# Rotary queries and keys projected once for four heads, halves placed by DMA, probabilities scaled on VectorE

## The chip, the cores and the metric

The kernel runs on one core of a Trainium2 chip. Its engines are TensorE (PE, with its weight loads as PEld), VectorE (DVE), ScalarE (ACT), GpSimd (POOL) and SyncE (SP, which issues DMAs); each works through its own instructions in order and waits on semaphores. The metric is the time of one execution on the device in microseconds (us).

## The reference

A decoder layer over x of shape (8, 256, 128): self-attention, cross-attention to a context of 1601 tokens, then a block with rotary attention and a mixture of 31 experts. The change is in the rotary attention alone. Cut to it:

```python
H, HD = (16, 64)
xn = _rmsnorm(x, gamma1)
q = (xn @ q_w + q_b).reshape(b, s, H, HD).transpose(0, 2, 1, 3)
k = (xn @ k_w + k_b).reshape(b, s, H, HD).transpose(0, 2, 1, 3)
v = (xn @ v_w + v_b).reshape(b, s, H, HD).transpose(0, 2, 1, 3)
# _rope: angles = arange(s)[:, None] * theta
x1, x2 = (x[..., 0::2], x[..., 1::2])
concatenate([x1 * cos - x2 * sin, x1 * sin + x2 * cos], axis=-1)   # for q and for k
scores = einsum('bhqd,bhkd->bhqk', q, k) / sqrt(HD)     # causal
attn = softmax(scores, axis=-1)
ctx = einsum('bhqk,bhkd->bhqd', attn, v)
attn_out = ctx @ o_w + o_b + xn
```

There are 8 batches of 256 tokens and 16 heads of 64 columns; everything here is float32.

## The kernel before

The program is a sequence of stages, each a block with one instruction stream per engine: self-attention, cross-attention, rotary attention (`rotary_attention`, from L1449), the gates, and the experts. The tables of sines and cosines (`RotaryTables`, L218) and the reordered weights are prepared during the self-attention stage.

In the rotary stage a unit is a pair of heads, `UN` = 8 units to a batch, 64 in all. The order is written out: `program` (L1493) calls `slot` for each engine once per unit, and within a slot each engine works on several units at different stages, set by the lags of L1433: the projection of the slot's own unit, the scores of the unit two slots back, its normalisation three back, its transposes four back, and its values five back. Slots 1 to 3 of a batch also carry the three parts of the norm of the next batch (`ahead`), slot 5 the output product of the batch before (item "o"), slot 6 its end on VectorE (`finish`), and slots 1, 2, 6 and 7 one piece each of the values' projection (item "v").

What the engines do for a unit:

- TensorE projects (L1764): queries and keys, each with the weights `w1` and with `w2`, where even and odd columns have changed places, 128 rows (two heads) by 256 tokens. Each of these 4 matmuls is 2 passes in the trace, 8 in all.
- VectorE (L1631) adds the bias and multiplies each of the four by the table: four products of 256 columns, from PSUM.
- GpSimd (L1554, L1557) adds them in pairs into `qT` and `kT`.
- TensorE makes the scores and adds the mask (L1723, L1726); VectorE takes the row maxima (L1607, L1608); ScalarE makes the exponentials and their sums (L1666); VectorE the reciprocals (L1613).
- GpSimd scales the probabilities by the reciprocals, four instructions over `prob` (L1548), one slot before TensorE transposes them (L1752). ScalarE copies the transposes (L1677), TensorE multiplies by the values (L1742), ScalarE copies the result (L1672).

In a slot TensorE's order is: "v" item, scores, "o" item, values, transposes, projection. SP issues nothing in this stage after the loads of the experts' first weights.

## Time and profile before

| | us |
|---|---|
| median of 3 runs (1802.65 to 1806.12) | 1804.21 |
| the profiled execution | 1805.63 |
| its span | 1803.6 |
| TensorE matmul busy | 1581.4 (88%) |
| VectorE busy | 1118.3 (62%) |
| ScalarE busy | 905.3 (50%) |
| GpSimd busy | 556.2 (31%) |

The profile shows one execution. Busy time is summed over the whole span, and the stages differ: the rotary stage lies between about 1132 and 1535 us of it. What a change in it is worth is read from the waits and the timeline of that stage.

### The profile page before, as it was taken

The page shows a single profiled execution, that of the slowest core. Times are in us where ns is not written, and L with a number is a line of the kernel's source. Part 1 is how long each engine was busy: PE and PEld are TensorE (multiplying, and loading weights), DVE is VectorE, ACT ScalarE, POOL GpSimd, SP SyncE. Part 2 cuts the span into 40 slices and gives each one's busy share as a digit, 9 for nine tenths or more (in the row PEclk, how much of TensorE's full clock was granted, in tenths as well). Part 3 has the DMA queues.
Part 4 walks back from the last instruction along what each step waited for, and adds up shares of the span by engine and source line. Part 5 has one row for each costly group of instructions (what it writes and reads, how often), then busy time and mean ns, then how long its engine had stood idle before and what let it go on. Part 6 is the DMA issues. An engine that isn't in the chain of part 4 may idle for free. (4 is left out here: it accounts for less than half of the span.)

```text
span 1803.6 us, 29464 instructions
## 1 busy us (share of the span) xinstructions
PE 1581.4 (88%) x11021; PEld 845.3 (47%) x11045; DVE 1118.3 (62%) x2537; ACT 905.3 (50%) x1612; POOL 556.2 (31%) x690
## 2 busy tenths in 40 slices
PE   1677776699999999999999999799999997499999
PEld 1344443244444444444444444466666675344444
DVE  4755542577778686868777784556666663355554
ACT  1233333076666667676666667255555554234333
POOL 4010102020111203030302000577888885133332
PEclk9978886599999999999999999899999998599999
DMA  4222211603232323223222320000000000000001
GB/s 102 69 51 54 54 37 55 114 5 93 47 96 47 97 47 96 47 77 52 63 53 43 97 33 2 8 1 2 1 1 1 1 1 1 7 20 22 22 19 36
DMA packets 88417, 75.32 MB, mean 42 GB/s; under 512 B 24724, under 2 KB 78388, under 8 KB 87348
## 3 DMA queue, kind: packets, MB, share of 16 engines
q1 hardware_dynamic: 88276, 73.44, 18.5%
q8 instruction: 88, 1.44, 0.3%
q14 instruction: 53, 0.43, 0.1%
HBM read 42.73 MB, written 30.42 MB: 41 GB/s over the span
## 5 line engine op out<-in xcount | busy, mean ns | idle before, releaser
L1137 DVE TENSOR_REDUCE b_chunk_max<-psum 128x1 f32<-128x400 f32 (+1 forms) x1024 | 545.4, 570 | 206.4 <-PE psum L1352 199.0
L1275 ACT ACTIVATE b_prob<-psum 128x1024 f32<-128x1024 f32 (+1 forms) x416 | 425.6, 1023 | 238.5 <-PE psum L1389 234.4
L1352 PE MATMUL psum<-k_stack,q_stack 128*128 128x400 bf16 (+1 forms) x1024 | 318.3, 345 | 31.2 <-DMA k_stack<-b_k_scratch 12.2
L1361 PE MATMUL psum<-b_prob,b_v_aug 128*32 128x256 f32 (+1 forms) x3328 | 266.1, 391 | 1.8 <-ACT b_prob L1275 0.5
L1389 PE MATMUL psum<-q_stack,k_stack 128*128 128x256 bf16 (+1 forms) x1664 | 253.0, 275 | 0.3 <-DMA q_stack<-b_mparts 0.3
L1389 PEld LDWEIGHTS psum<-q_stack,k_stack 128*128 128x128 bf16 (+1 forms) x1664 | 146.3, 99 | 118.1 <-issue 51.2
L1548 POOL TENSOR_SCALAR c_prob<-c_prob,c_rec 128x128 f32<-128x128 f32 (+1 forms) x256 | 191.9, 767 | 8.9 <-POOL c_kT L1557 8.3
L2027 DVE TENSOR_TENSOR e_hg<-e_gl,e_gate 128x512 f32<-128x512 f32 x128 | 123.9, 986 | 113.0 <-PE psum L2042 69.3
L1352 PEld LDWEIGHTS psum<-k_stack,q_stack 128*128 128x128 bf16 x1024 | 99.2, 97 | 201.7 <-DVE b_chunk_max L1137 170.5
L1631 DVE SCALAR_TENSOR_TENSOR c_turned<-psum,c_bias,c_tab 128x256 f32<-128x256 f32 x256 | 106.1, 476 | 111.1 <-PE psum L1764 111.1
L1666 ACT ACTIVATE c_prob<-psum,c_mneg 128x128 f32<-128x128 f32 (+1 forms) x256 | 104.1, 418 | 136.4 <-DVE c_mneg L1608 136.4
L2008 ACT ACTIVATE e_gl<-psum,b1T 128x512 f32<-128x512 f32 x128 | 87.8, 687 | 139.8 <-PE psum L2055 131.6
L2042 PE MATMUL psum<-e_hg,e_w 128*128 128x512 f32 x256 | 131.9, 598 | 8.6 <-DVE e_hg L2027 8.6
L2055 PE MATMUL psum<-anT,e_w 128*128 128x512 f32 x256 | 133.3, 604 | 1.4 <-PEq L1813 1.4
L1764 PE MATMUL psum<-c_xT,c_w 128*128 128x256 f32 x512 | 130.6, 401 | 1.7 <-DVE c_turned L1631 1.2
L1993 POOL PARTITION_BROADCAST e_gate<-e_gate_row x32 | 73.8, 2311 | 174.4 <-DMA e_gate_row<-gates 139.9
L1071 POOL COPY b_v_aug<-b_v_new 128x768 f32<-128x768 f32 (+1 forms) x32 | 15.9, 528 | 335.1 <-issue 268.5
L1361 PEld LDWEIGHTS psum<-b_prob,b_v_aug 128*32 128x32 f32 (+1 forms) x3328 | 65.8, 108 | 105.4 <-issue 86.7
L1764 PEld LDWEIGHTS psum<-c_xT,c_w 128*128 128x128 f32 x512 | 98.1, 202 | 15.4 <-DVE c_turned L1631 2.5
L578 DVE TENSOR_REDUCE a_mneg<-psum 128x2 f32<-128x512 f32 (+1 forms) x96 | 65.0, 688 | 58.9 <-PE psum L752 57.6
L653 ACT ACTIVATE a_prob<-psum 128x1024 f32<-128x1024 f32 x64 | 51.8, 811 | 72.1 <-PE psum L723 70.9
L2042 PEld LDWEIGHTS psum<-e_hg,e_w 128*128 128x128 f32 x256 | 49.0, 192 | 71.0 <-issue 52.8
(213 smaller groups left out, 1961.6 us busy)
## 6 DMA issues: line engine op xcount, KB each, us to landing
k_stack<-b_k_scratch SPq DMA_DIRECT2D x32, 600.4 KB, 10.5
b_k_scratch<-b_kparts SPq DMA_DIRECT2D x7, 1200.8 KB, 4.3
b_k_scratch<-b_kparts SPq DMA_DIRECT2D x7, 800.5 KB, 6.0
b_ctx<-in_ctx SPq DMA_DIRECT2D x8, 576.0 KB
e_w<-in_L_ffn_re_w SPq DMA_DIRECT2D x62, 64.0 KB, 1.9
a_scratch<-a_parts SPq DMA_DIRECT2D x16, 192.0 KB, 2.2
k_stack<-a_scratch SPq DMA_DIRECT2D x16, 192.0 KB, 4.9
q_stack<-b_q_scratch SPq DMA_DIRECT2D x32, 96.0 KB, 2.2
```

Source lines behind the costliest of these rows:

```text
L1137: nc.vector.tensor_reduce(out=chunk_max[:, half, q, column4(hh), c:c + 1], in_=psum[:, 2 + u % 2, 0:w], axis=AX.X, op=ALU.max).then_inc(ma ...
L1275: nc.scalar.activation(prob[0:k, buf, :].rearrange("p (a c) -> p a c", a=2), psum[0:k, 4 + 2 * buf:6 + 2 * buf, :], ACT.Exp, scale=HD ** - ...
L1352: nc.tensor.matmul(psum[:, 2 + u % 2, 0:hi - lo], queries_of(qst, h, slice(q * P, q * P + P)), keys_of(kst, h, slice(lo, hi)), start=True, ...
L1361: last = nc.tensor.matmul(pv[32 * hh:32 * hh + 32, :], v_aug[0:k, kt, g * GH + hh, :], prob[0:k, buf, c:c + T], start=(kt == 0), stop=(kt ...
L1389: lastmm = nc.tensor.matmul(psum[0:k, 4 + 2 * buf + hh % 2, (hh // 2) * T:(hh // 2) * T + T], keys_of(kst, h, slice(n * P, n * P + k)), qu ...
L1548: ins = nc.gpsimd.tensor_scalar(prob[:, w % PB, hh, lo:hi], prob[:, w % PB, hh, lo:hi], rec[:, w % PB, hh, q:q + 1], None, ALU.mult)
L1631: ins = nc.vector.scalar_tensor_tensor(out=turned[:, u % 2, m, w, :], in0=bank[:, w * T:(w + 1) * T], scalar=bias[:, m, w, u:u + 1], in1=t ...
L1666: ins = nc.scalar.activation(prob[:, u % PB, hh, lo:hi], psum[:, 2 + hh, lo:hi], ACT.Exp, bias=mneg[:, par, q, hh:hh + 1], accum_out=total ...
L1764: last = nc.tensor.matmul(bank[:, w * T:(w + 1) * T], weights[:, m, u * P:(u + 1) * P], xT[:], start=True, stop=True)
L2027: nc.vector.tensor_tensor(hg[:, k % BUFS, :], gl[:, k % BUFS, :], gate[j][:, c * TW:(c + 1) * TW], ALU.mult)\
L2042: nc.tensor.matmul(psum[:, c, :], w[:, j, 1, :], hg[:, buf, :], start=second.start, stop=False).then_inc(y_done, 1)
L2055: nc.tensor.matmul(psum[:, 4 + k % BUFS, :], w[:, j, 0, :], d["anT"][:, c * TW:(c + 1) * TW], start=True, stop=True)\
```

## The change

A unit of the projection is now queries (even units) or keys (odd units) of four heads: one matmul gives the first columns of the four heads' pairs (`half` 0), one the second (`half` 1), 32 columns a head. The weights and biases come in this order from the host, so the copies on GpSimd (`order_weights`) and the small bias loads are gone. VectorE makes four products out of the two projections (first times cosine, second times sine, first times sine, second times cosine). GpSimd adds the last two into `second` and subtracts the first two twice, into two slots of `qT` or `kT` that take two heads each. Half of the rows written there belong to the other slot's heads; SP's four DMAs of 32 rows put the `second` halves in their place. The scores of a unit wait for the DMAs of queries and keys of its four heads (`placed`) and come three slots after the projection instead of two. The reciprocals and the scaling of the probabilities are both on VectorE, at the start of the slot in which TensorE transposes them.

```diff
-        self.w1, self.w2 = sb("c_w1", [P, 2, CH * CD]), sb("c_w2", [P, 2, CH * CD])
+        self.w = sb("c_w", [P, 2, UN // 2, 2, P])
...
-        for q in range(0, P, 64):
-            link(nc.vector.tensor_scalar(tab[q:q + 32, 1, 1, :], tab[q:q + 32, 1, 1, :], -1.0, None, ALU.mult))
...
-                tables.order_weights(pool)
-
...
-SCORES_LAG, NORM_LAG, TURN_LAG, VALUES_LAG = 2, 3, 4, 5
+SCORES_LAG, TURN_LAG, VALUES_LAG = 3, 4, 5
...
@@ -1513,6 +1496,13 @@
         @block.sync
         def _(sp):
             experts_pre.load(sp)
+            for n in range(B * UN):
+                m, u, buf = n % 2, n % UN // 2 * 2, n % 2
+                sp.wait_ge(turned_ready, n + 1)
+                for pos in range(4):
+                    to = 32 * (pos ^ 1)
+                    sp.dma_start((qT, kT)[m][to:to + 32, u + pos % 2, :], second[32 * pos:32 * pos + 32, buf, :])\
+                        .then_inc(placed[m], 16)
@@ -1539,24 +1529,24 @@
-                w = c_unit(n, NORM_LAG, first, drain)
-                if w is not None:
-                    pool.wait_ge(rec_ready, T_.up("weigh"))
-                    pool.sem_inc(passed, 1)
-                    for hh in range(2):
-                        for lo, hi, q in ((0, P, 0), (P, 3 * P, 1)):
-                            ins = nc.gpsimd.tensor_scalar(prob[:, w % PB, hh, lo:hi], prob[:, w % PB, hh, lo:hi],
-                                                          rec[:, w % PB, hh, q:q + 1], None, ALU.mult)
-                    ins.then_inc(weighed, 1)
                 if u is not None:
-                    pool.wait_ge(terms_ready, T_.up("unit"))
-                    par = u % 2
-                    nc.gpsimd.tensor_tensor(qT[:, u, :], turned[:, par, 0, 0, :], turned[:, par, 0, 1, :], ALU.add)\
-                        .then_inc(own_pool, 1)
+                    v = T_.up("unit")
+                    pool.wait_ge(terms_ready, v)
+                    m, g, t4 = u % 2, u // 2 * 2, terms[:, u % 2]
+                    if v > UN:
+
+                        pool.wait_ge(s_full, (v - 1) // 2 * 2 + 2 - UN)
+                    if v > 2:
+
+                        pool.wait_ge(placed[m], 64 * ((v - 1) // 2))
+                    nc.gpsimd.tensor_tensor(second[:, m, :], t4[:, 2, :], t4[:, 3, :], ALU.add).then_inc(own_pool, 1)
                     pool.wait_ge(own_pool, T_.up("own_pool"))
-                    nc.gpsimd.tensor_tensor(kT[:, u, :], turned[:, par, 1, 0, :], turned[:, par, 1, 1, :], ALU.add)\
-                        .then_inc(turned_ready, 1)
-                    pool.wait_ge(turned_ready, T_.now("unit"))
+                    for j in range(2):
+                        nc.gpsimd.tensor_tensor((qT, kT)[m][:, g + j, :], t4[:, 0, :], t4[:, 1, :], ALU.subtract)\
+                            .then_inc((own_pool, turned_ready)[j], 1)
+                        if j == 0:
+                            pool.wait_ge(own_pool, T_.up("own_pool"))
+                    pool.wait_ge(turned_ready, v)
@@ -1600,6 +1590,16 @@
             def slot(i, n, first, drain, ahead):
+                u = c_unit(n, TURN_LAG, first, drain)
+                if u is not None:
+                    dve.wait_ge(exp_done, T_.up("weigh"))
+                    own(nc.vector.reciprocal(rec[:, u % PB].rearrange("p h q -> p (h q)"),
+                                             total[:, u % PB].rearrange("p h q -> p (h q)")))
+                    for hh in range(2):
+                        for lo, hi, q in ((0, P, 0), (P, 3 * P, 1)):
+                            ins = nc.vector.tensor_scalar(prob[:, u % PB, hh, lo:hi], prob[:, u % PB, hh, lo:hi],
+                                                          rec[:, u % PB, hh, q:q + 1], None, ALU.mult)
+                    ins.then_inc(weighed, 1)
...
-                    for m, bank in enumerate((q_bank, k_bank)):
-                        for w in range(2):
-                            ins = nc.vector.scalar_tensor_tensor(out=turned[:, u % 2, m, w, :], in0=bank[:, w * T:(w + 1) * T],
-                                                                 scalar=bias[:, m, w, u:u + 1], in1=tab[:, m, w, :],
-                                                                 op0=ALU.add, op1=ALU.mult)
+                    m, bank = u % 2, (q_bank, k_bank)[u % 2]
+                    for dst, (half, wave) in enumerate(((0, 0), (1, 1), (0, 1), (1, 0))):
+                        ins = nc.vector.scalar_tensor_tensor(out=terms[:, m, dst, :], in0=bank[:, half * T:(half + 1) * T],
+                                                             scalar=bias[:, m, u // 2, half:half + 1], in1=tab[:, m, wave, :],
+                                                             op0=ALU.add, op1=ALU.mult)
                     ins.then_inc(terms_ready, 1)
@@ -1715,7 +1710,9 @@
-                    pe.wait_ge(turned_ready, T_.up("scores"))
+                    quads = (T_.up("scores") + 1) // 2
+                    pe.wait_ge(placed[0], 64 * quads)
+                    pe.wait_ge(placed[1], 64 * quads)
@@ -1758,11 +1755,11 @@
-                    wait(pe, terms_ready, T_.now("unit", 1))
-                    for m, bank in enumerate((q_bank, k_bank)):
-                        for w, weights in enumerate((w1, w2)):
-                            last = nc.tensor.matmul(bank[:, w * T:(w + 1) * T], weights[:, m, u * P:(u + 1) * P], xT[:],
-                                                    start=True, stop=True)
+                    wait(pe, terms_ready, T_.now("unit", 2))
+                    bank = (q_bank, k_bank)[u % 2]
+                    for half in range(2):
+                        last = nc.tensor.matmul(bank[:, half * T:(half + 1) * T], qkw[:, u % 2, u // 2, half, :], xT[:],
+                                                start=True, stop=True)
                     last.then_inc(proj_full, 1)
```

VectorE before, one plain slot of the rotary stage, from the products of one unit (`c_turned`) to those of the next; `c_mneg` holds the negated row maxima, `c_rec` the reciprocals:

```order
L1631 SCALAR_TENSOR_TENSOR c_turned<-psum,c_bias,c_tab 128x256 [waits c_turned_ready,c_proj_full]
L1631 SCALAR_TENSOR_TENSOR c_turned<-psum,c_bias,c_tab 128x256 x3
L1607 TENSOR_REDUCE c_mneg<-psum 128x2 [waits c_s_full]
L1608 TENSOR_REDUCE c_mneg<-psum 128x2
L1613 RECIPROCAL c_rec<-c_total 128x4 [waits c_exp_done]
L1631 SCALAR_TENSOR_TENSOR c_turned<-psum,c_bias,c_tab 128x256 [waits c_turned_ready,c_proj_full]
L1631 SCALAR_TENSOR_TENSOR c_turned<-psum,c_bias,c_tab 128x256 x3
```

VectorE after, the same place (`c_terms` are the four products, `c_prob` the probabilities):

```order
L1626 SCALAR_TENSOR_TENSOR c_terms<-psum,c_bias,c_tab 128x256 [waits c_turned_ready,c_proj_full]
L1626 SCALAR_TENSOR_TENSOR c_terms<-psum,c_bias,c_tab 128x256 x3
L1596 RECIPROCAL c_rec<-c_total 128x4 [waits c_exp_done]
L1600 TENSOR_SCALAR c_prob<-c_prob,c_rec 128x128 [waits c_own_dve]
L1600 TENSOR_SCALAR c_prob<-c_prob,c_rec 128x256
L1600 TENSOR_SCALAR c_prob<-c_prob,c_rec 128x128
L1600 TENSOR_SCALAR c_prob<-c_prob,c_rec 128x256
L1607 TENSOR_REDUCE c_mneg<-psum 128x2 [waits c_s_full]
L1608 TENSOR_REDUCE c_mneg<-psum 128x2
L1626 SCALAR_TENSOR_TENSOR c_terms<-psum,c_bias,c_tab 128x256 [waits c_turned_ready,c_proj_full]
L1626 SCALAR_TENSOR_TENSOR c_terms<-psum,c_bias,c_tab 128x256 x3
```

The reciprocal has moved in front of the row maxima, and four scalings stand between it and them.

TensorE before, a slot from the scores (`c_kT,c_qT`) and the mask over the values (`c_probT,c_v`) and the transposes (`ident,c_prob`) to the projection (`c_xT,c_w`):

```order
L1723 MATMUL psum<-c_kT,c_qT 128x128 [waits c_exp_done,c_turned_ready]
L1723 MATMUL psum<-c_kT,c_qT 128x128
L1723 MATMUL psum<-c_kT,c_qT 128x256 x2
L1726 MATMUL psum<-mask_qk,identb 128x2x128 x2
L1742 MATMUL psum<-c_probT,c_v 64x256 [waits c_att_ready,c_probT_ready]
L1742 MATMUL psum<-c_probT,c_v 64x256
L1742 MATMUL psum<-c_probT,c_v 64x128 x2
L1752 MATMUL psum<-ident,c_prob 128x128 [waits c_probT_ready,c_weighed]
L1752 MATMUL psum<-ident,c_prob 128x128 x5
L1764 MATMUL psum<-c_xT,c_w 128x256 [waits c_terms_ready]
L1764 MATMUL psum<-c_xT,c_w 128x256 x3
```

TensorE after, the same place:

```order
L1720 MATMUL psum<-c_kT,c_qT 128x128 [waits c_exp_done,c_k_placed,c_q_placed]
L1720 MATMUL psum<-c_kT,c_qT 128x128
L1720 MATMUL psum<-c_kT,c_qT 128x256 x2
L1723 MATMUL psum<-mask_qk,identb 128x2x128 x2
L1739 MATMUL psum<-c_probT,c_v 64x256 [waits c_att_ready,c_probT_ready]
L1739 MATMUL psum<-c_probT,c_v 64x256
L1739 MATMUL psum<-c_probT,c_v 64x128 x2
L1749 MATMUL psum<-ident,c_prob 128x128 [waits c_probT_ready,c_weighed]
L1749 MATMUL psum<-ident,c_prob 128x128 x5
L1761 MATMUL psum<-c_xT,c_w 128x256 [waits c_terms_ready]
L1761 MATMUL psum<-c_xT,c_w 128x256
```

The order of the groups stays. The scores wait for the two `placed` semaphores, and the projection has two matmuls instead of four.

## Rows read from the trace of the kernel before

**Rows 1.** Busy time by windows, a batch: stretch, its length, each engine, granted clock, DMA.
```profile
1374.00:1420.00 46.00, 42.69 (x292) 30.36 (x294) 28.91 (x87) 24.70 (x85) 37.64 (x54) 1.00 0.00 1
```

**Rows 2.** Waits from 1200 to 1480: who for whom, us in total, times, longest.
```profile
DVE c_turned L1631 <- PE psum L1764: 84.1, 37, 5.2
```

**Rows 3.** The projection: its timeline row in slot 4, then all of its passes.
```profile
1160.34 1.89 PE L1764 MATMUL psum<-c_xT,c_w 128*128 128x256 f32 x8
...
L1764 PE MATMUL psum<-c_xT,c_w x512: 378/379/795, 1139.2 to 1504.5; 128*128 128x256 f32 x171
```

**Rows 4.** Timeline, slots 4 and 5: start, duration, engine, line, operation, count [idle before].
```profile
1296.73 1.66 DVE L1631 SCALAR_TENSOR_TENSOR c_turned<-psum,c_bias,c_tab 128x256 f32<-128x256 f32 x4 [5.02 <-PE psum L1764]
...
1298.48 0.72 POOL L1554 TENSOR_TENSOR c_qT<-c_turned 128x256 f32<-128x256 f32 x1 [0.46 <-DVE c_turned L1631]
...
1298.71 0.87 PE L1752 MATMUL psum<-ident,c_prob 128*128 128x128 f32 x6
...
1299.42 1.89 PE L1764 MATMUL psum<-c_xT,c_w 128*128 128x256 f32 x8
...
1301.24 0.93 PE L1723 MATMUL psum<-c_kT,c_qT 64*128 64x128 f32 x8
...
1301.35 1.66 DVE L1631 SCALAR_TENSOR_TENSOR c_turned<-psum,c_bias,c_tab 128x256 f32<-128x256 f32 x4 [1.94 <-PE psum L1764]
...
1302.33 3.74 PE L1704 MATMUL psum<-c_ow,c_attT 128*128 128x128 f32 x32
1302.92 0.41 DVE L1607 TENSOR_REDUCE c_mneg<-psum 128x2 f32<-128x256 f32 x1
...
1303.85 0.17 DVE L1613 RECIPROCAL c_rec<-c_total 128x4 f32<-128x4 f32 x1
1303.97 0.37 ACT L1666 ACTIVATE c_prob<-psum,c_mneg 128x128 f32<-128x128 f32 x1 [1.83 <-DVE c_mneg L1608]
...
1305.48 0.21 ACT L1666 ACTIVATION_READ_ACCUMULATOR c_prob<-psum,c_mneg 128x1 f32 x1
...
1305.99 0.87 PE L1742 MATMUL psum<-c_probT,c_v 128*64 128x256 f32 x8
```

**Rows 5.** Timeline, norm scalings beside GpSimd's adds; then the two apart (ns min/median/max).
```profile
1285.46 0.73 POOL L1554 TENSOR_TENSOR c_qT<-c_turned 128x256 f32<-128x256 f32 x1
...
1285.95 1.13 DVE L127 TENSOR_SCALAR xn<-x_sb,mv,rstd 128x128 f32<-128x128 f32 x2
...
1286.26 0.73 POOL L1557 TENSOR_TENSOR c_kT<-c_turned 128x256 f32<-128x256 f32 x1
...
L127 DVE TENSOR_SCALAR xn<-x_sb,mv,rstd x2: 324/602/881, 1285.9 to 1286.2; 128x128 f32<-128x128 f32 x2
```

**Rows 6.** Groups by line and form: a 256-column multiplication by a per-partition scalar.
```profile
L303 DVE TENSOR_SCALAR t_ang<-t_pos,c_theta 128x256 f32<-128x256 f32 x2 | 0.7, 354 | 0.1
```

**Rows 7.** Timeline, four small DMAs and who waits for them; then issues by size.
```profile
1106.84 2.37 SPq L994 DMA_DIRECT2D q_stack<-b_mparts  x4
...
1110.27 0.61 PE L1389 MATMUL psum<-q_stack,k_stack 128*128 128x256 bf16 x4 [0.32 <-DMA q_stack<-b_mparts]
...
a_scratch<-a_parts SPq DMA_DIRECT2D x16, 192.0 KB, 2.2
```

**Rows 8.** Timeline, VectorE: last of the norm's second part; first and last of a batch's end.
```profile
1288.44 0.17 DVE L142 TENSOR_SCALAR ve<-msq 128x2 f32<-128x2 f32 x1
...
1312.50 1.23 DVE L149 SCALAR_TENSOR_TENSOR an_cur<-c_o,rstd,c_rows 128x128 f32<-128x128 f32 x2
...
1314.60 0.65 DVE L1587 TENSOR_TENSOR x_sb<-x_sb,c_o 128x256 f32<-128x256 f32 x1
```

**Rows 9.** Timeline after a gap of TensorE; then a window as in rows 1.
```profile
1292.55 0.87 PE L1752 MATMUL psum<-ident,c_prob 128*128 128x128 f32 x6 [2.35 <-POOL c_prob L1548]
...
1293.26 3.43 PE L1764 MATMUL psum<-c_xT,c_w 128*128 128x256 f32 x8
...
262.50:269.00 6.50, 3.94 (x43) 1.87 (x42) 3.69 (x10) 2.34 (x5) 0.00 (x0) 1.00 0.00 1
```

More of the change, by code:

```diff
@@ L249, in scratch @@
     def scratch(self, sb):
-        self.raw = sb("t_raw", [P, 2, CH * CD])
         self.pos, self.posi = sb("t_pos", [P, T]), sb("t_posi", [P, T], mybir.dt.int32)
@@ L256, in load @@
         nc, a = self.nc, self.a
-        for m, name in enumerate(("q_w", "k_w")):
-            sp.dma_start(self.raw[:, m, :], a["L0_ffn_" + name]).then_inc(self.loaded, 16)
-        with nc.allow_non_contiguous_dma(reason="biases are spread over partitions once"):
-            for quarter in range(4):
-                rows = slice(32 * quarter, 32 * quarter + 32)
-                sp.dma_start(self.theta[rows, :], a["L0_ffn_theta"].rearrange("(p a) -> p a", a=1)).then_inc(self.loaded, 16)
-                hh, par = quarter // 2, quarter % 2
-                for m, name in enumerate(("q_b", "k_b")):
-                    v = a["L0_ffn_" + name].rearrange("(j h f a) -> h a f j", j=UN, h=2, a=2)
-                    for w in range(2):
-                        sp.dma_start(self.bias[rows, m, w, :], v[hh, (par + w) % 2]).then_inc(self.loaded, 16)
-    N_LOADS = 2 + 4 * 5
+        for m, name in enumerate(("q", "k")):
+            sp.dma_start(self.w[:, m].rearrange("p g a n -> p (g a n)"), a["L0_ffn_%s_w" % name]).then_inc(self.loaded, 16)
+            sp.dma_start(self.bias[:, m].rearrange("p g a -> p (g a)"), a["L0_ffn_%s_b" % name]).then_inc(self.loaded, 16)
+        for quarter in range(4):
+            rows = slice(32 * quarter, 32 * quarter + 32)
+            sp.dma_start(self.theta[rows, :], a["L0_ffn_theta"].rearrange("(p a) -> p a", a=1)).then_inc(self.loaded, 16)
+    N_LOADS = 2 * 2 + 4
     def positions(self, pool):
         self.nc.gpsimd.iota(self.posi[:], pattern=[[1, T]], base=0, channel_multiplier=0).then_inc(self.pos_set, 1)
-    def order_weights(self, pool):
-        pool.wait_ge(self.loaded, 16 * self.N_LOADS)
-        for m in range(2):
-            v = self.raw[:, m, :].rearrange("p (g f a) -> p g a f", g=CH, a=2)
-            for par in range(2):
-                for dst, src in ((self.w1, par), (self.w2, 1 - par)):
-                    self.nc.gpsimd.tensor_copy(dst[:, m, :].rearrange("p (g a f) -> p g a f", g=CH, a=2)[:, :, par], v[:, :, src])
     def angles(self, dve):
@@ L1461, in sem @@
             return ctx.enter_context(nc.semaphore(name))
-        w1, w2, tab, bias = tables.w1, tables.w2, tables.tab, tables.bias
+        qkw, tab, bias = tables.w, tables.tab, tables.bias
         vw, ow, rows, vbT, w_loaded = tables.vw, tables.ow, tables.rows, tables.vbT, tables.w_loaded
@@ L1466, in rotary_attention @@
         o = sb("c_o", [P, QT, D])
-        turned = sb("c_turned", [P, 2, 2, 2, T])
+        terms = sb("c_terms", [P, 2, 4, T])
+        second = sb("c_second", [P, 2, T])
         qT = sb("c_qT", [P, UN, T])
@@ L1487, in rotary_attention @@
         misc, pv_bank = psum[:, 6, :], psum[:, 7, :]
-        PER = dict(unit=UN, scores=UN, weigh=UN, turn=UN, values=UN, item=6, batch=1, norm=3, out=1, own_pool=UN,
-                   own_dve=(NORM_LINKS + RMS_LINKS) + RMS_LINKS + 3)
+        PER = dict(unit=UN, scores=UN, weigh=UN, turn=UN, values=UN, item=6, batch=1, norm=3, out=1, own_pool=2 * UN,
+                   own_dve=(NORM_LINKS + RMS_LINKS) + RMS_LINKS + 3 + UN)
         N_W = tables.N_W
@@ L1609, in slot @@
                         .then_inc(m_ready, 1)
-                u = c_unit(n, NORM_LAG, first, drain)
-                if u is not None:
-                    dve.wait_ge(exp_done, T_.up("weigh"))
-                    nc.vector.reciprocal(rec[:, u % PB].rearrange("p h q -> p (h q)"), total[:, u % PB].rearrange("p h q -> p (h q)"))\
-                        .then_inc(rec_ready, 1)
                 ahead()
@@ L2093 @@
     for name in _NAMES:
-        v = _np.ascontiguousarray(inputs[name])
+        v = _np.asarray(inputs[name])
+        if name in ("L0_ffn_q_w", "L0_ffn_k_w"):
+            v = v.reshape(D, 4, 2, 2, 32, 2).transpose(0, 1, 5, 3, 2, 4).reshape(D, CH * CD)
+        if name in ("L0_ffn_q_b", "L0_ffn_k_b"):
+            v = v.reshape(4, 2, 2, 32, 2).transpose(2, 1, 3, 0, 4).reshape(P, UN)
+        v = _np.ascontiguousarray(v)
         arrays["in_" + name] = v
```

6 lines of the change are left out of this document (3 added, 3 removed).

## The prediction

> **What bounds the kernel now.** I read the page first: TensorE is the busiest engine and the stages follow each other, so a change in one stage is worth what it does there. The changed lines run in the rotary stage. The table by windows shows a batch of it: of 46.0 us TensorE is busy 42.69, VectorE 28.91, GpSimd 37.64, at a full clock [rows 1]. The table of waits says the same from the other side: VectorE waits for the projection 84.1 us in 280 [rows 2], so it has room on average. From the first projection of the steady stretch (slot 4 of the first batch) to the last one, whose eighth pass starts at 1504.5, are 1504.5 - 1.5 - 1160.3 = 343 us for 59 slots, 5.8 us a slot [rows 3]. TensorE sets that; GpSimd, which scales the probabilities a whole slot before they are transposed, is nearly hidden.
>
> The timeline of single slots then gives the pieces [rows 4]: transposes 0.71 us until the projection starts (1298.71 to 1299.42); projection 1.89 for 8 passes, with 0.378 for one by itself [rows 3], so (1.89 - 0.378) / 7 = 0.216 a pass; VectorE starts 0.04 after it and needs 1.66 for its four products; GpSimd starts 0.09 after those; scores and mask 1.09 (1301.24 to 1302.33), output product 3.66 (to 1305.99), values 0.87; row maxima 1.0 (1302.92 until the exponentials start); reciprocal 0.17; exponentials 1303.97 to 1305.69, 1.7.
>
> **What the change takes away.** Half of the projection: 4 passes of 8 in each of 64 slots, 4 x 0.216 = 0.86 us a slot, 55 us of TensorE's path. GpSimd loses four scalings a slot and gets a third add. In the self-attention stage GpSimd's reordering of the weights goes, which stood beside VectorE's work there; I estimate 1 us for it.
>
> **What it adds: a loop of one slot.** Before, the scaling of a unit was done in the slot before its transposes. Now it is in the same slot, on VectorE, in front of the row maxima and the products; TensorE's transposes wait for it, and the projection stands behind the transposes (both orders are shown above). So each slot runs around: products of slot n-1 end, scaling, transposes, projection of slot n, products of slot n. No engine can run ahead of this. Outside the scaling it costs 0.06 (a wake, estimated between the 0.04 and 0.09 above) + 0.71 + projection 3 x 0.216 + 0.378 = 1.03 + 0.04 + 1.66 = 3.5 us.
>
> The scaling by itself: a 128-column scaling by per-partition scalars takes 0.32 at least [rows 5], a 256-column one 0.354 [rows 6]; 2 x (0.32 + 0.354) = 1.35, with the reciprocal 1.5 us. Bounds for it alone: 1.1 (if the pieces overlap as the row maxima do) and 1.9 (if a 256-column piece ran at the products' 1.66 / 4 = 0.42 and small ones too). Alone, the loop is 5.0 us.
>
> It isn't alone. GpSimd's three adds start 0.09 us after the products end, which is when VectorE goes on to the scaling. What happens when a scaling from SBUF meets GpSimd adds stands in one place of the trace: two equal scalings, 0.324 and 0.881 us; the first ends at 1286.27, just behind the add that ended at 1286.19; the second ends at 1287.08, behind the add of 1286.26 to 1286.99 [rows 5]. The adds kept their 0.73. So the scaling waits for the whole add and gets in between two. The Trainium skill has this as a rule (SBUF — State Buffer, Who interferes with whom): one port pair is shared by VectorE and GpSimd and is locked for a whole instruction. The trace agrees with it here; without such a lock the sum would be that of the first rival.
>
> With three adds at a pitch of 0.80 (ends at 0.82, 1.62 and 2.42 after the products), three scalings end at some 0.9, 1.7 and 2.5, and the fourth is free: 2.5 + 0.35 = 2.9 us. Loop: 2.9 + 3.5 = 6.4 us. Bounds: 5.0 (never in the way) and 7.3 (all four behind the last add: 2.42 + 1.35 = 3.8 instead of 2.9). I take 6.4, by the row. The exponentials are ready: they end 1.7 after the maxima, the products 1.66 after them at the earliest.
>
> **The transfers.** Four DMAs of 32 KB start when the third add ends, 2.42 after the products; the scores two slots on wait for them, in every odd slot. Four small DMAs issued together take 1106.84 to 1110.27, 3.4 us, until TensorE goes on [rows 7]; one alone takes 2.2 from issue to landing [rows 7]. For 32 KB each I take 3.6 for all four. Ready 6.1 us after the products; scores 1.09 and values 0.87 bring the transposes to 8.1. The scaling of that slot lets them go at 6.4 + 2.9 = 9.3. So the transfers are hidden by the locked loop, except where the output product (3.66, slot 5) stands between: 6.1 + 1.09 + 3.66 + 0.87 = 11.7, 2.3 us late, once a batch. If the loop were the short one, this wait would take its place.
>
> **VectorE's other work.** Between maxima and products there is 0.06 + 0.71 + 1.03 + 0.04 - 1.0 = 0.8 us of room. The second part of the norm took 1285.95 to 1288.61, the end of a batch 1312.50 to 1315.25 [rows 8], each with about 0.6 of the same lock in it, which no longer falls there: 2.1 and 2.15, so 1.3 and 1.35 stand out. The shorter items fit.
>
> **The sum.** A batch: 8 x 6.4 + 2.3 + 1.3 + 1.35 = 56.2 us, 8 x 5.8 = 46.5 now. The 59 slots are 7 batches and 3 plain slots: 7 x 56.2 + 3 x 6.4 = 412.6, less 343 is 70 us. Filling is a little shorter and draining has one more slot of scores, which waits for a transfer: together I estimate +2. Stage A -1. Together +71. The profiled execution took 1805.6 us for a span of 1803.6, 1.4 over the median of 1804.2; on the median I forecast 1804.2 + 71 = **1875 us**. The 55 us taken off TensorE turn into idle time of TensorE.
>
> **First rival: no lock, the transfers bind.** Loop 5.0, but in odd slots the transposes start at 8.1 instead of 5.0 + 1.5 = 6.5. A pair of slots: 8.1 + 0.71 + 1.03 + 0.04 + 1.66 = 11.5; a batch 4 x 11.5 + 3.66 = 49.8; 7 x 49.8 + 3 x 5.8 = 366, +23: with fill, drain and stage A +24, **1828**. For it: only one clear meeting of the two kinds of instruction is in the trace. Against it: that one is exact to 0.1 us.
>
> **Second rival, on the other side.** No lock, and four transfers land like one, in 2.2 us. Place: the scores of odd slots. Ready at 4.7, transposes at 6.7; a pair is 10.1, a batch 44.1 and some 0.9 for the long items; 7 x 45 + 3 x 5.0 = 330, -13, with the rest -12: **1792**. It decides only if no lock and a landing under some 2.6 us come together: at 2.6 a pair is 10.5, and 4 x 10.5 + 3.66 + 0.9 are the present 46.5 us. Were even the loop wrong and TensorE still the bound, all 55 us would come: 1750; both orders speak against that.
>
> **Third rival: the clock.** TensorE would be busy 3.8 of 6.4 us, with gaps of 1 to 1.7 us. After the 2.35 us gap at 1290.2 the next 8 passes took 3.43 instead of 1.89, so it had fallen to the lower of its levels, 1.2 GHz [rows 9]. Against it: 6.5 us with 3.94 busy went at a full clock [rows 9]. At the low level the loop gets 0.71 + 1.03 = 1.7 us longer and the output product 3.7: some 130 us if always so; TensorE would then be busy over 7 of 8.1 us, which should bring the clock back, so I count half: **1940**. [...]
>
> **How the numbers follow.** Locked loop at a full clock: 55%, own range 1855 to 1900. No lock: 20%. Clock: 17%. The fast one: 4%. The rest, 4%, lies around no change, when errors of a microsecond a slot in the loop add up. The range of 8 in 10 reaches from 1820 (the first rival with its width) to 1940. About 0.2% (3.6 us) is what a measurement of this kernel can tell from no change: faster 4%, within it 2%, slower 94%.
>
> **What would show it.** In the profile after: slots of the rotary stage at 6.4 us and a batch at 56; TensorE's transposes idle before them, released by VectorE's scaling, once a slot; VectorE's products waiting for the projection about 0.8 us in plain slots; the four scalings together 2.5 us or more while the adds keep 0.73 (first step); the projection at 4 passes in 1.03; TensorE's scores released by a transfer only in slot 5. If the scalings take 1.4 together, the lock is wrong and the scores of odd slots will be waiting for transfers. If the granted clock of the stage is under 0.9, the third rival has its part. The forecast is wrong if the transposes don't wait for the scaling at all.

## The result, and the profile after

The changed kernel takes 1870.55 us (median of 4 runs, 1869.59 to 1870.9); the kernel before, run beside it, 1805.16 (1802.65 to 1808.79). The ratio is 1.036, 95% interval 1.0341 to 1.0379: 3.6% slower, 65 us. The forecast was 1875. (One execution of one later kernel, with the projection ahead of the transposes, took 3020.89 us in the slow state; its ratio leaves that one out.)

The profiled span is 1868.7 us, 65.1 more than before. The rotary stage has nearly all of it. From the projection of slot 4 of the first batch, which starts at 1157.84, to the last one, at 1563.95, are 406.1 us for 59 slots, against 343 [rows 3]: +63. Slot 4 itself comes 2.5 us earlier (1160.34 before), and from the start of the last projection to the gates' first transposes it is 36.7 us (to 1600.63) instead of 32.3 (1503.03 to 1535.36).

Two windows of the profile after, columns as in rows 1; the first is one batch, from the start of one output product to the next:

```profile
1436.38:1491.01 54.63, 40.41 (x267) 27.28 (x267) 43.43 (x120) 24.96 (x85) 22.21 (x29) 0.94 0.07 20
...
1170.00:1500.00 330.00, 244.44 (x1590) 165.48 (x1592) 260.04 (x712) 149.53 (x510) 132.63 (x173) 0.93 0.07 20
```

This batch takes 54.6 us instead of 46; the six between the output products at 1212.54 and 1545.34 take 54.0 to 57.7, 55.5 in the mean. TensorE idles 14 us of the batch shown and VectorE has become the busier engine. The granted clock of the stage is 0.93, where the same window of the kernel before has 0.98. From the costliest groups and the DMA issues of the page:

```profile
L1720 PE MATMUL psum<-c_kT,c_qT 64*128 64x128 f32 (+1 forms) x512 | 65.1, 374 | 84.9 <-DMA c_kT<-c_second 75.7
...
L1749 PE MATMUL psum<-ident,c_prob 128*128 128x128 f32 x384 | 63.7, 309 | 34.8 <-DVE c_prob L1600 34.6
...
c_qT<-c_second SPq DMA_DIRECT2D x128, 32.0 KB, 1.8
```

TensorE waits for both new things: 35 us in front of the transposes for the scaling, and 76 us in front of the scores for the transfers, where the forecast had such a wait in slot 5 alone. The forms of the scaling apart, from 1170 to 1500 (busy us, mean ns):

```profile
L1600 DVE TENSOR_SCALAR c_prob<-c_prob,c_rec 128x128 f32<-128x128 f32 x95 | 72.5, 764 | 1.7
L1600 DVE TENSOR_SCALAR c_prob<-c_prob,c_rec 128x256 f32<-128x256 f32 x94 | 32.1, 341 | 0.0
```

The 128-column scaling takes over twice as long as the 256-column one that follows it: the time is a wait. The timeline, slots 7 and 0, then the first half of a locked scaling block of another batch taken apart, then slots 1 and 3 to 5 (start, duration, count, idle before):

```profile
1455.23 1.66 DVE L1626 SCALAR_TENSOR_TENSOR c_terms<-psum,c_bias,c_tab 128x256 f32<-128x256 f32 x4 [0.91 <-PE psum L1761]
...
1457.01 2.02 DVE L1600 TENSOR_SCALAR c_prob<-c_prob,c_rec 128x128 f32<-128x128 f32 x4
...
1460.86 1.66 DVE L1626 SCALAR_TENSOR_TENSOR c_terms<-psum,c_bias,c_tab 128x256 f32<-128x256 f32 x4 [0.90 <-PE psum L1761]
...
1322.84 0.82 DVE L1600 TENSOR_SCALAR c_prob<-c_prob,c_rec 128x128 f32<-128x128 f32 x1
1322.85 0.72 POOL L1542 TENSOR_TENSOR c_second<-c_terms 128x256 f32<-128x256 f32 x1 [3.04 <-DVE c_terms L1626]
...
1322.84 1.08 DVE L1600 TENSOR_SCALAR c_prob<-c_prob,c_rec 128x128 f32<-128x128 f32 x2
1323.65 0.85 POOL L1545 TENSOR_TENSOR c_qT<-c_terms 128x256 f32<-128x256 f32 x1
...
1463.37 0.93 PE L1720 MATMUL psum<-c_kT,c_qT 64*128 64x128 f32 x8 [1.69 <-DMA c_kT<-c_second]
...
1466.99 1.72 PE L1761 MATMUL psum<-c_xT,c_w 128*128 128x256 f32 x4
...
1476.83 0.93 PE L1720 MATMUL psum<-c_kT,c_qT 64*128 64x128 f32 x8 [2.55 <-DMA c_kT<-c_second]
...
1479.88 1.03 PE L1761 MATMUL psum<-c_xT,c_w 128*128 128x256 f32 x4
...
1480.95 1.66 DVE L1626 SCALAR_TENSOR_TENSOR c_terms<-psum,c_bias,c_tab 128x256 f32<-128x256 f32 x4 [0.38 <-PE psum L1761]
...
1485.30 2.41 SPq L1504 DMA_DIRECT2D c_kT<-c_second  x4
...
1486.52 1.66 DVE L1626 SCALAR_TENSOR_TENSOR c_terms<-psum,c_bias,c_tab 128x256 f32<-128x256 f32 x4 [0.91 <-PE psum L1761]
...
1489.03 1.65 PE L1720 MATMUL psum<-c_kT,c_qT 64*128 64x128 f32 x8 [2.54 <-DMA c_kT<-c_second]
...
1491.01 4.34 PE L1699 MATMUL psum<-c_ow,c_attT 128*128 128x128 f32 x32
...
1496.80 1.03 PE L1761 MATMUL psum<-c_xT,c_w 128*128 128x256 f32 x4
...
1497.87 1.66 DVE L1626 SCALAR_TENSOR_TENSOR c_terms<-psum,c_bias,c_tab 128x256 f32<-128x256 f32 x4 [0.33 <-PE psum L1761]
```

The reader is to see three things. A plain slot is 1460.86 - 1455.23 = 5.63 us. Its four scalings go in two pairs: the first, which starts with the add, ends at 1323.66, 0.09 us behind it, and the second is through 0.26 later, at 1323.92. The record of the next add starts at 1323.65 already, but it takes 0.85 us instead of 0.73, so part of it is a wait too. And slot 5 takes 1497.87 - 1486.52 = 11.35 us, because the transfers of its unit, issued at 1485.30, let the scores go at 1489.03 only; the projection's 4 passes there, and in plain slots, take the 1.03 of the forecast. The scores in that slot (1.65) and the output product (4.34, 3.74 before [rows 4]), and transposes and projection of slot 1 (1.54, and 1.72 as shown, against 0.87 and 1.03), ran partly or wholly at TensorE's lower level, 1.2 GHz, each after a wait for a transfer (1.69 us in slot 1, 2.54 in slot 5). The wait of 2.55 us in slot 3 left the clock at full: the projection behind it takes 1.03.

### The profile page after: what moved, and what is told of

Same layout as the page of the kernel before. It is cut to its first block and busy times, and to the rows that moved or that the text cites. A ratio compares the mean times of both kernels' runs of the same rounds, so it can differ in the third digit from the quotient of the medians.

```text
span 1868.7 us, 29303 instructions
## 1 busy us (share of the span) xinstructions
PE 1558.5 (83%) x10789; PEld 815.2 (44%) x10789; DVE 1229.2 (66%) x2791; ACT 903.2 (48%) x1612; POOL 421.6 (23%) x490
## 5 line engine op out<-in xcount | busy, mean ns | idle before, releaser
L1626 DVE SCALAR_TENSOR_TENSOR c_terms<-psum,c_bias,c_tab 128x256 f32<-128x256 f32 x256 | 106.1, 476 | 55.8 <-PE psum L1761 55.8
L1720 PE MATMUL psum<-c_kT,c_qT 64*128 64x128 f32 (+1 forms) x512 | 65.1, 374 | 84.9 <-DMA c_kT<-c_second 75.7
L1600 DVE TENSOR_SCALAR c_prob<-c_prob,c_rec 128x128 f32<-128x128 f32 (+1 forms) x256 | 123.8, 543 | 2.2
L1749 PE MATMUL psum<-ident,c_prob 128*128 128x128 f32 x384 | 63.7, 309 | 34.8 <-DVE c_prob L1600 34.6
L1720 PEld LDWEIGHTS psum<-c_kT,c_qT 64*128 64x128 f32 x512 | 37.7, 200 | 119.6 <-issue 102.4
```

The source lines that it names most:

```text
L1600: ins = nc.vector.tensor_scalar(prob[:, u % PB, hh, lo:hi], prob[:, u % PB, hh, lo:hi], rec[:, u % PB, hh, q:q + 1], None, ALU.mult)
L1626: ins = nc.vector.scalar_tensor_tensor(out=terms[:, m, dst, :], in0=bank[:, half * T:(half + 1) * T], scalar=bias[:, m, u // 2, half:half ...
L1720: nc.tensor.matmul(psum[:, 2 + hh, q * P:q * P + w], qT[r, u, q * P:q * P + P], kT[r, u, 0:w], start=(q == 0), stop=False, tile_position=( ...
```

## The experiments

My theory after the result had three parts: a loop of one slot through the scaling, the lock between VectorE's scalings and GpSimd's adds in it, and the transfers with the low clock behind their waits. Its rivals: that the transfers are hidden, that one part alone has the whole loss, and that any rotation of the loop's order would give the time back. All ratios are to the kernel before, run on the same chip.

**No transfers.** SP issues none, and the scores wait for the adds. The second halves of queries and keys are thus not put in place; everything else is computed.

```diff
-                for pos in range(4):
-                    sp.dma_start((qT, kT)[m][to:to + 32, ...], second[...]).then_inc(placed[m], 16)
...
-                    if v > 2:
-                        pool.wait_ge(placed[m], 64 * ((v - 1) // 2))
...
-                    pe.wait_ge(placed[0], 64 * quads)
-                    pe.wait_ge(placed[1], 64 * quads)
+                    pe.wait_ge(turned_ready, 2 * quads)
```

> The changed kernel without SyncE's four transfers a slot: the second halves are not put in place, so the scores are computed from other numbers; they wait for GpSimd's adds instead. Loop theory (scaling, transposes, projection, products, with the scaling waiting for GpSimd's adds: 5.62 us a slot in the trace of the changed kernel): slots stay at 5.6, but the waits of odd slots and half of the slot with the output product go: a batch 54.6 -> some 49.6, time about 1833. Rival 1, the transfers are hidden (as my forecast had it): no more than 2.3 us a batch, 1853 or above. Rival 2, the transfers bind everything: a slot goes under 5.2, time 1810 or below. If TensorE's clock had fallen because of the waits, the granted clock of the stage rises from 0.93 to 0.98 or more.

Measured: 1825.05 us, ratio 1.0102 (1.0078 to 1.0126), 45 us under the changed kernel. So the transfers were not hidden. Without their waits the granted clock from 1170 to 1500 is 0.98, as in the kernel before. The timeline shows the plain slot unchanged, 5.62 to 5.63:

```profile
1375.16 1.66 DVE L1616 SCALAR_TENSOR_TENSOR c_terms<-psum,c_bias,c_tab 128x256 f32<-128x256 f32 x4 [0.90 <-PE psum L1750]
...
1380.79 1.66 DVE L1616 SCALAR_TENSOR_TENSOR c_terms<-psum,c_bias,c_tab 128x256 f32<-128x256 f32 x4 [0.90 <-PE psum L1750]
```

Of the waits from 1170 to 1500 the scaling's is left alone on TensorE's path, where the changed kernel had 53.0 us for the keys' transfers and 27.6 for the scaling:

```profile
PE psum L1738 <- DVE c_prob L1590: 50.6, 47, 1.8
```

**No transfers, and the adds after the scaling.** As in the last kernel, and GpSimd waits until VectorE's scaling of the slot is done, so that the two never meet.

```diff
+                    if v > 3:
+                        pool.wait_ge(weighed, v - 3)
                     nc.gpsimd.tensor_tensor(second[:, m, :], t4[:, 2, :], t4[:, 3, :], ALU.add)
```

> As no_transfers, and GpSimd's adds of a slot wait until VectorE has done its scalings, so the two never meet. Scores are again computed without the second halves in place. Lock theory: the four scalings take 1.3 instead of 2.0 us, the loop 5.0 instead of 5.6, a batch about 46, time about 1807, 26 us under no_transfers. Rival (no lock, the scalings are slow by themselves): scalings stay at 2.0, time as no_transfers or above it.

Measured: 1783.78, ratio 0.9875 (0.9852 to 0.9898). The lock is worth 41 us of the other kernel's time, more than I expected. The 128-column form, and the timeline:

```profile
L1592 DVE TENSOR_SCALAR c_prob<-c_prob,c_rec 128x128 f32<-128x128 f32 x121 | 34.3, 284 | 2.1
```

```profile
1349.84 1.66 DVE L1618 SCALAR_TENSOR_TENSOR c_terms<-psum,c_bias,c_tab 128x256 f32<-128x256 f32 x4 [0.90 <-PE psum L1752]
...
1351.62 1.01 DVE L1592 TENSOR_SCALAR c_prob<-c_prob,c_rec 128x128 f32<-128x128 f32 x4
...
1354.60 1.66 DVE L1618 SCALAR_TENSOR_TENSOR c_terms<-psum,c_bias,c_tab 128x256 f32<-128x256 f32 x4 [1.04 <-PE psum L1752]
```

Without adds beside them the four scalings take 1.01 us, not 2.02, and the slot 4.76 (4.64 for the next one). The 128-column scaling falls from 766 to 284 ns; the 256-column one takes 348 and took 341.

**The projection ahead of the transposes.** The two groups change places in TensorE's stream, which takes scaling and transposes out of the loop from products to products. The edit in outline:

```diff
-   transposes (waits for weighed); projection (waits for terms_ready)
+   projection (waits for terms_ready); transposes (waits for weighed)
```

> The changed kernel, complete, with TensorE's projection ahead of its transposes in every slot. Loop theory: products of a slot no longer wait for the scaling and the transposes, the one-slot loop is gone; what is left is the pair loop over the transfers: adds end 2.7 after the products, transfers 3.7, scores and values 2.0, projection 1.0, products 1.7, that is 11.1 for two slots; a batch 4 x 11.1 + 3.7 = 48, time about 1822. Rival (the loop was never the bound, only the transfers): 0.7 us less in each odd slot, 3 us a batch, about 1848. If the clock keeps falling, 10 to 20 us more in either.

Measured: 1866.52, ratio 1.0328 (1.0299 to 1.0358), 4 us better than the changed kernel by the medians and hardly more than their spread. The loop theory's 1822 is missed, with 10 to 20 us for the clock too. The rival's 1848 with the same 10 to 20 reaches it (the granted clock from 1170 to 1500 is 0.90), but not for its reason, since in the kernels without transfers the loop does bind. So the rival that a rotation of the order gives the time back is refuted for this one. TensorE's timeline shows why:

```profile
1392.69 0.95 PE L1720 MATMUL psum<-c_kT,c_qT 64*128 64x128 f32 x8 [2.23 <-DMA c_kT<-c_second]
...
1394.11 1.55 PE L1739 MATMUL psum<-c_probT,c_v 128*64 128x256 f32 x8
1395.59 1.75 PE L1752 MATMUL psum<-c_xT,c_w 128*128 128x256 f32 x4
```

The projection of the next slot stands in the same stream behind scores that wait for a transfer. What the shorter loop gives is spent there, and behind each wait TensorE runs slower (1.55 and 1.75 instead of 0.87 and 1.13). In this kernel it waited 66.8 us of 330 for the keys' transfers, against 53.0 in the changed one.

**The kernel before, with the scaling alone moved to VectorE** (in the slot between scores and transposes, ahead of the row maxima as in the change; projection, adds and lags are those of before). In outline:

```diff
-                        nc.gpsimd.tensor_scalar(prob[...], prob[...], rec[...], None, ALU.mult)
+   in VectorE's slot, ahead of the row maxima, of the unit 3 slots back:
+                            ins = nc.vector.tensor_scalar(prob[...], prob[...], rec[...], None, ALU.mult)
```

> The kernel before with one part of the change alone: the scaling is done by VectorE, at the start of the slot before the transposes, so no loop closes over it. Loop theory: VectorE gets some 2 us a slot more work, 4.9 x 8 + 7 = 46 us a batch, just as much as TensorE; time within 1795 to 1815. Rival (the scaling on VectorE costs by itself, wherever it stands): 1850 or above.

Measured: 1835.3, ratio 1.0162 (1.0131 to 1.0194): about 29 us slower, and outside my range of up to 1815; the rival's 1850 was not reached either. The scaling has the same lock here, and it stands in front of the row maxima, for which the exponentials wait, and for these the next scores:

```profile
1329.68 2.03 DVE L1601 TENSOR_SCALAR c_prob<-c_prob,c_rec 128x128 f32<-128x128 f32 x4
...
1332.67 0.37 ACT L1662 ACTIVATE c_prob<-psum,c_mneg 128x128 f32<-128x128 f32 x1 [3.15 <-DVE c_mneg L1609]
...
1334.54 0.93 PE L1719 MATMUL psum<-c_kT,c_qT 64*128 64x128 f32 x8 [1.62 <-ACT c_prob L1662]
```

So this part of the change costs time by itself, even where the transposes come a slot later. That halving the projection cannot give it back while the loop is there is argued from the loop, not tried by itself.

**One more slot of lag.** The changed kernel with scores, transposes and values 4, 5 and 6 slots after the projection, and the items moved to fit. It computes all that the changed kernel does.

```diff
-SCORES_LAG, TURN_LAG, VALUES_LAG = 3, 4, 5
+SCORES_LAG, TURN_LAG, VALUES_LAG = 4, 5, 6
-C_ITEMS = {1: [("v", 0)], 2: [("v", 1)], 5: [("o", 0)], 6: [("v", 2)], 7: [("v", 3)]}
+C_ITEMS = {2: [("v", 0)], 3: [("v", 1)], 6: [("v", 2), ("o", 0)], 7: [("v", 3)]}
```

> The changed kernel, complete, with scores, transposes and values one slot later (4, 5, 6 instead of 3, 4, 5; the pieces of the values' projection and the output product move along). The loop over the scaling and its meeting with GpSimd's adds stay; the transfers get a slot more. Transfer theory: as without the transfers (1825), plus one slot of draining: about 1830, slots at 5.6, no wait of the scores for a transfer. Rival (the four transfers cost something else than the wait, traffic or SyncE): 1850 or above.

Measured: 1830.96, ratio 1.0151 (1.0122 to 1.0179), the expected time within 1 us. I had expected no wait of the scores for a transfer; for the keys' transfers 11.6 us of 53.0 are left in the stretch 1170 to 1500 (second row), while the scaling holds the transposes as before (first row):

```profile
PE psum L1747 <- DVE c_prob L1600: 51.1, 47, 1.8
...
PE psum L1718 <- DMA c_kT<-c_second: 11.6, 17, 1.0
```

**The same, and the adds after the scaling** (`pool.wait_ge(weighed, v - 4)` ahead of them, for v over 4).

> As lag4, and GpSimd's adds wait for VectorE's scalings of the slot, complete. If waits for transfers and the lock were the whole loss: as no_transfers_late_adds (1784) plus a slot of draining and items at another place, about 1790, below the kernel before. Rival (later adds make the transfers late again: adds end 3.6 after the products, ready at 7.3, scores wanted at 9 to 10): the scores of odd slots wait, 1800 or above.

Measured: 1786.26, ratio 0.9906 (0.9876 to 0.9936). This is the fastest complete kernel, 0.9% faster than the kernel before and some 84 us faster than the changed one. Now TensorE's scores wait for a transfer 1.9 us in the stretch (second row), and for the exponentials instead:

```profile
PE psum L1720 <- ACT c_prob L1661: 32.4, 37, 1.9
...
PE psum L1720 <- DMA c_kT<-c_second: 1.9, 4, 0.9
```

**The same, and the projection ahead of the transposes**, to see whether the rotation helps once nothing else binds.

> As lag4_late_adds, with TensorE's projection ahead of its transposes. Now no transfer and no lock stands before the loop, so loop theory says that this is where the order matters: the plain slot falls from 4.6 to VectorE's own work, 0.2 + 1.3 + 1.0 + 1.7 = 4.1 us, a batch by 2 to 4 us, time about 1770. Rival (project_first gave 4 us, so the order doesn't matter here either): within 5 us of lag4_late_adds.

Measured: 1792.24, ratio 0.9929 (0.9905 to 0.9952), 6 us behind the last one instead of 16 ahead; the rival's 5 us is missed too, narrowly. TensorE's timeline:

```profile
1405.10 2.08 PE L1752 MATMUL psum<-c_xT,c_w 128*128 128x256 f32 x4
...
1419.65 0.93 PE L1720 MATMUL psum<-c_kT,c_qT 64*128 64x128 f32 x8 [1.90 <-ACT c_prob L1661]
...
1424.58 0.93 PE L1720 MATMUL psum<-c_kT,c_qT 64*128 64x128 f32 x8 [1.15 <-ACT c_prob L1661]
```

Scores here follow scores by 4.93 us (1419.65 to 1424.58), both times released by the exponentials of the unit before, which read the same PSUM banks: once the projection's loop is open, this one (scores, maxima with the scaling ahead of them, exponentials, scores) holds the slot at the same length; the last kernel has 4.93 for it too (1416.45 to 1421.38). Behind the wait of 1.90 us that ends at 1402.83 projection and transposes took 2.08 and 1.26 instead of 1.13 and 0.82; the granted clock from 1170 to 1450 is 0.96 against 1.00 for the last kernel, which may be what put this one behind it. That the banks are what holds was read, not tried, and the clock's part is argued only.

**The scaling back on GpSimd** in the changed kernel, a slot ahead of the transposes as before (lags 3, 4, 5, 6; items and output product move along as in the kernels with one more slot). In outline:

```diff
-   VectorE: reciprocals and four scalings at the start of the slot
+   VectorE: reciprocals; GpSimd: the four scalings of the unit 4 slots back, ahead of its adds
```

> The changed kernel with the second part of the change undone: GpSimd scales the probabilities, four slots behind the projection, transposes five and values six behind (a slot later than in the changed kernel, as the order before had it); scores stay at three. Transfer theory: the pair loop over the transfers stays (adds 2.4, transfers 3.7, scores and values 2.0, transposes 0.7, projection 1.0, products 1.7: 11.5 for two slots), 50 a batch, about 1825 to 1835. Lock theory alone (all of the loss is VectorE's scaling): back at 1805 or below, the projection's saving would show.

Measured: 1888.51, ratio 1.0466 (1.0438 to 1.0494), far from 1825 to 1835.

```profile
1414.71 1.65 DVE L1628 SCALAR_TENSOR_TENSOR c_terms<-psum,c_bias,c_tab 128x256 f32<-128x256 f32 x4
...
1414.74 2.98 POOL L1538 TENSOR_SCALAR c_prob<-c_prob,c_rec 128x128 f32<-128x128 f32 x4 [0.23 <-POOL c_qT L1554]
...
1417.69 0.73 POOL L1551 TENSOR_TENSOR c_second<-c_terms 128x256 f32<-128x256 f32 x1
...
1420.05 2.41 SPq L1504 DMA_DIRECT2D c_kT<-c_second  x4
...
1423.78 1.65 PE L1722 MATMUL psum<-c_kT,c_qT 64*128 64x128 f32 x8 [4.27 <-issue]
```

VectorE is free, but the adds, whose products are done at 1416.36, stand behind a 3 us scaling on GpSimd until 1417.69. The transfers are issued 3.7 us after the products instead of 2.7, the scores start 3.73 later, and TensorE idles 4.27 us (which the profile puts down to no wait that it shows) and then runs at its lower level: the scores take 1.65, and the granted clock from 1170 to 1500 is 0.86. I had priced the scaling by VectorE's loop alone and forgotten what it does to the transfers behind it.

**TensorE kept busy during the waits.** The changed kernel with matmuls nobody reads in front of the wait of every even unit.

```diff
+                    wait(pe, exp_done, T_.now("scores", 1))
+                    if u % 2 == 0:
+                        for _ in range(36):
+                            nc.tensor.matmul(psum[:, 2, 3 * P:4 * P], t["identb"][:], t["identb"][:], start=True, stop=True)
                     pe.wait_ge(placed[0], 64 * quads)
                     pe.wait_ge(placed[1], 64 * quads)
-                    wait(pe, exp_done, T_.now("scores", 1))
```

> The changed kernel, with 36 extra matmuls (128 columns, bf16, into columns that nobody reads) ahead of TensorE's wait for the transfers in every even unit, so that it is busy for most of that wait; the result is unchanged. Clock theory: after the changed kernel's waits of 2.6 us the output product took 5.37 us instead of 3.7, transposes and projection of slot 1 3.3 instead of 1.9, some 3 to 4 us a batch. With TensorE busy these go: granted clock of the stage 0.97 or more, output product 3.7, batch 51, in all 1870 - 8 x 3.3 = about 1845. The waits for the transfers themselves stay (slot 5 still +2.3). Rival: the gaps are not what lowers the clock, or the extra matmuls themselves keep the scores waiting: no change or slower, 1868 to 1880.

Measured: 1862.79, ratio 1.0322 (1.0298 to 1.0346), 8 us under the changed kernel (7 by the ratios). That lies between the theory's 1845 and the rival's 1868. Its window from 1170 to 1500, then TensorE and SP in slot 5:

```profile
1170.00:1500.00 330.00, 281.35 (x2535) 201.97 (x2532) 270.25 (x737) 153.15 (x523) 138.00 (x179) 1.00 0.08 21
```

```profile
1318.56 2.41 SPq L1504 DMA_DIRECT2D c_kT<-c_second  x4
...
1320.69 2.18 PE L1717 MATMUL psum<-identb 128*128 128x128 bf16 x36 [0.94 <-ACT c_prob L1661]
1322.81 0.93 PE L1723 MATMUL psum<-c_kT,c_qT 64*128 64x128 f32 x8
...
1323.89 3.74 PE L1699 MATMUL psum<-c_ow,c_attT 128*128 128x128 f32 x32
```

The clock theory holds as to the mechanism, and its price of 25 us was too high: with the gaps filled the stage is granted 1.00, and the output product takes 3.74 again. The filler isn't free: it ends at 1322.87, while transfers issued at 1318.56 were usable 3.7 us later, at 1322.3, so it holds the scores back some 0.5 us. The 8 us are therefore a lower bound for what the clock costs. In slot 3 the scores still wait 1.51 us behind the filler, so at most 3 times 0.5 us a batch comes on top, which makes about 8 to 20 us, an estimate.

**The adds after the scaling, with the lags of the change.**

```diff
+                    if v > 3:
+                        pool.wait_ge(weighed, v - 3)
```

> The changed kernel, with its lags and transfers, but GpSimd's adds of a unit wait until VectorE's scaling of that slot is done. The lock is gone (scalings 1.4 us for the four, adds 0.73), but the adds end some 1.3 us later (3.7 instead of 2.4 us after the products), and so do the transfers, which the scores of the even units wait for. Theory that the transfers bind as much as the lock: transfers ready 7.4 us after the products, +1.09 + 0.87 to the transposes, +0.71 + 1.03 + 0.04 + 1.66 to the next products, 12.8 us for a pair of slots instead of 11.2, 50.6 + 3.7 a batch or more, with the clock as low as now: 1865 to 1885. Rival (the lock is what counts, as in the kernels without transfers, where the same edit gave 41 us): 1830 to 1845.

Measured: 1935.13, ratio 1.0725 (1.0699 to 1.075): 65 us slower than the changed kernel. The rival, that the lock is what counts, is wrong; my own sum gave at most 15 us more than the changed kernel and was 50 us short. From the products of one unit (which end at 1331.52) to those two slots on:

```profile
1329.86 1.66 DVE L1628 SCALAR_TENSOR_TENSOR c_terms<-psum,c_bias,c_tab 128x256 f32<-128x256 f32 x4 [1.56 <-PE psum L1763]
...
1335.25 2.41 SPq L1504 DMA_DIRECT2D c_kT<-c_second  x4
...
1338.99 1.65 PE L1722 MATMUL psum<-c_kT,c_qT 64*128 64x128 f32 x8 [4.55 <-DMA c_kT<-c_second]
...
1341.11 1.41 PE L1741 MATMUL psum<-c_probT,c_v 128*64 128x256 f32 x8
...
1344.23 1.66 DVE L1628 SCALAR_TENSOR_TENSOR c_terms<-psum,c_bias,c_tab 128x256 f32<-128x256 f32 x4 [1.47 <-PE psum L1763]
```

The transfers are ready 1338.99 - 1331.52 = 7.47 us after the products (7.4 expected), but scores, mask and values then take 3.5 us instead of 2.0, at the low clock: a pair of slots is 14.37 instead of 12.8. Output products of this kernel start 63.3 us apart (1228.86 to 1545.39 for five), which is 4 x 14.4 and one output product of 5.7.

Put together, ratios to the kernel before:

| | adds at once (lock) | adds after the scaling |
|---|---|---|
| scores 3 slots after, with transfers | 1.036 | 1.0725 |
| scores 4 slots after, with transfers | 1.0151 | 0.9906 |
| scores 3 slots after, no transfers | 1.0102 | 0.9875 |

Two costs of some 40 to 47 us each, lock and exposed transfers, and they are tied: taking the lock away by later adds pays only where the transfers have room.

## Why the prediction was right, and where it wasn't

**The one-slot loop** was right, and was the main thing. The transposes wait for the scaling in every plain slot, VectorE's products wait about 0.9 us for the projection (0.8 predicted), and 3.5 us lie outside the scaling: 5.63 less the 2.14 from the end of the products (1456.89) to the end of the scaling (1459.03).

**The lock** was right, and its price too high. Predicted: one scaling gets in behind each add, the block ends 2.9 us after the products, the loop is 6.4 us. Measured: two get in behind each add, the block ends 2.14 after, the loop is 5.63. The row that I used [rows 5] has two scalings of one size, and only the second shows a wait: the first took 0.324, the least of the 48 in that trace (median 0.340), though it started while the add still ran. Four in a row did not occur there. The adds did not keep their 0.73 either: those behind a pair of scalings took 0.85. The Trainium skill (SBUF — State Buffer, Who interferes with whom) says that whoever holds the shared ports has them for a whole instruction; the trace agrees as to the waiting, with 0.82 for a scaling that takes 0.28 alone, and adds that a second one can slip through before GpSimd's next add gets on. Alone, the block was mis-sized as well: 1.1 us after the products (loop of 4.64 to 4.76 without lock), which was my lower bound, not 1.5. The reciprocal starts before the products have ended and so costs almost nothing.

**The transfers** were well timed and wrongly called hidden. Predicted ready 6.1 us after the products, measured 1489.03 - 1482.61 = 6.42 (third add over 0.2 later; four transfers 3.7 from issue to use, 3.6 predicted). But "hidden" was worked out against a loop of 6.4 us. Against 5.63, two slots give them 5.63 + 2.14 = 7.77 until the transposes may go, and 6.42 + 1.09 + 0.87 = 8.38 is later. So every odd slot would be 0.6 late. Slots 3 and 7 of the batch shown are not, because the slot before each is lengthened by the norm and by the end of a batch. In slot 5 the term was 2.3 (2.4 by its own sum); with the real loop it is 3.95, with the 0.3 and 1.5 us of lower clock the 5.7 by which that slot exceeds a plain one. The sentence of the prediction that a shorter loop would let this wait take its place is what happened, in part.

**The batch.** Predicted 8 x 6.4 + 2.3 + 1.3 + 1.35 = 56.2. Measured, from slot 5 at 1443.25 to the next at 1497.87: 54.6, that is 8 x 5.63 = 45.0, slot 5 +5.7, slot 1 +2.3 (a transfer, and 1.4 us of low clock in transposes and projection), slot 2 +1.0 (the norm's second part), slot 6 +0.7 (the end of a batch). The lock's term is 6 us too high, the waits behind transfers and their clock 6 us too low, the items together 1 too high. Over all seven batches the mean is 55.6 ((406.1 - 3 x 5.63) / 7), with more low clock in some than in this one. That the total of 1875 came so near to 1870.55 is luck: it owes more to these cancelling than to its terms, and would be no basis for another kernel.

**The ends.** 59 slots: +70 predicted, +63 measured. Fill, drain and the self-attention stage together +1 predicted, +2 measured: the first transfer of the cross-attention's queries is issued at 349.6 instead of 352.0, so that stage is 2.3 us shorter, not 1 (that the removed copies give it was not tried apart); draining cost 4.3.

**The rivals.** Both without a lock fell with the scalings' 764 ns. The clock's rival has a part: 0.93 is above the 0.9 that I named as its sign, but filling the gaps brought it to 1.00 and 8 us back. My count of TensorE's gaps, 1 to 1.7 us, left out the waits for transfers, behind which it fell. The Trainium skill (TensorE: Matmul & The Clock Gate, HAM oscillation) describes a clock that falls again and again behind waits for DMAs, with waits of about 3 to 5 us in its example. The trace has it with shorter ones, and not behind each: of the 24 waits for the keys' transfers from 1170 to 1500, 10 of the 14 of 2.5 to 2.8 us and 4 of the 10 of 1.7 us were followed by work at the lower level, the others by work at full clock. How far the clock can go is seen in the kernel with late adds: 0.85 from 1170 to 1500, with waits of 4.5 us.

## What to carry to other kernels

Find the loop that a moved instruction closes before counting what the edit saves: here 55 us of TensorE's work went and the kernel got 65 us slower. A cost called hidden is hidden behind a certain duration; when that duration is an estimate, work the cover out for the low end of it too. And two costs that share a loop should be removed in the right order: first room for the transfers, then the lock, since the reverse order made it 65 us worse.
